# A graph network on one core: the matrix build tile by tile, two (later three) node ranges a tile, and relation weights and gathers moved

## The reference

```python
dst = jnp.minimum((6250 * jax.random.uniform(...) ** 2.0).astype(jnp.int32), 49999)   # then sorted
# layer 0: attention over the edges of a node, weighted by a relation weight
z = h @ W.T
rel_alpha = rel_emb[etype, 0]                       # 40 relations
h_agg = segment_sum((rel_alpha * alpha)[:, None] * z[src], dst)
# layer 1: mean over neighbours
summed = segment_sum(node_feature[src], dst)
# layer 2, three times: weighted sum over neighbours
agg = segment_sum(x[src] * w[:, None], dst);  out = agg @ W_rel.T + b_rel + x @ W_root.T
# layer 3: sum over neighbours of h[col] * mlp(edge_rbf)
```

## Time and profile before

| | us |
|---|---|
| median of 3 runs (lowest to highest) | 11397.75 (11381.71 to 11407.65) |
| the profiled execution | 11385.68 |
| its span, from the first to the last instruction | 11384.1 |

### The profile page before, as it was taken

One profiled execution on the slowest core, in us unless ns is written; L12 is line 12 of the kernel. 1 busy time (PEld: TensorE's weight loads), 2 busy tenths in 40 slices (PEclk: granted clock), 3 DMA queues, 4 the chain that ended last, 5 costly groups with the idle time before them and its releaser, 6 DMA issues. The chain is left out here.

```text
span 11384.1 us, 169604 instructions
## 1 busy us (share of the span) xinstructions
PE 7768.9 (68%) x40442; PEld 4847.1 (43%) x40443; DVE 4764.8 (42%) x10974; ACT 2337.1 (21%) x4276; POOL 4043.9 (36%) x4338
## 2 busy tenths in 40 slices
PE   1466666666666565555557999999977777777575
PEld 1222222222323354444443444444455555555565
DVE  7765554444333466555554357000121122222455
ACT  0001111222222455555541000000011111111000
POOL 2677776777661000000000000000047777777100
PEclk8899999999999756666668999999977777777899
DMA  1233444555554433222225777777733333333343
GB/s 48 70 105 125 137 147 161 170 183 183 192 193 154 136 113 104 96 92 89 84 81 199 282 279 289 282 289 287 294 111 116 117 119 117 118 116 113 122 139 123
DMA packets 537811, 1758.10 MB, mean 154 GB/s; under 512 B 96112, under 2 KB 286555, under 8 KB 494020
## 3 DMA queue, kind: packets, MB, share of 16 engines
q1 hardware_dynamic: 374136, 1331.26, 33.8%
q0 software_dynamic: 160032, 421.72, 12.0%
q10 hardware_dynamic: 3312, 1.94, 0.1%
HBM read 1223.40 MB, written 531.19 MB: 154 GB/s over the span
## 5 line engine op out<-in xcount | busy, mean ns | idle before, releaser
L849 PE MATMUL wide<-ring 128*128 x9424 | 2039.8, 342 | 1445.8 <-issue 891.0
L748 POOL DMA_INDIRECT z_got<-z_table,z_idx x1568 | 1837.9, 1172 | 698.6 <-issue 384.2
L849 PEld LDWEIGHTS wide<-ring 128*128 x9424 | 917.9, 97 | 2351.1 <-issue 2092.4
L1756 POOL DMA_INDIRECT sorted_rows<-l_rows,l_idx x1568 | 1553.9, 991 | 603.9 <-issue 439.9
L1384 PE MATMUL wide<-stream,X 128*128 128x512 f32 (+1 forms) x2548 | 1042.2, 569 | 60.1 <-DMA stream<-c_dense 57.9
L385 PE MATMUL wide<-rows,onehot 128*128 128x130 f32 x3904 | 877.1, 413 | 226.0 <-DVE A L402 225.7
L793 DVE TENSOR_TENSOR ring<-iota_h,src_r 128x512 bf16<-128x512 f16 (+1 forms) x394 | 272.7, 692 | 1720.0 <-PE wide L849 1702.7
L1003 POOL DMA_DIRECT2D rows<-z_edges x196 | 103.4, 528 | 2399.5 <-PE wide L374 2069.3
L1645 PE MATMUL wide<-H,l_onehot_t 128*128 x3904 | 547.5, 275 | 595.9 <-DVE l_rows L1718 529.1
L385 PEld LDWEIGHTS wide<-rows,onehot 128*128 128x128 f32 x3904 | 808.7, 314 | 289.0 <-DVE A L402 285.9
L1384 PEld LDWEIGHTS wide<-stream,X 128*128 128x128 f32 x2548 | 467.4, 191 | 600.6 <-issue 540.2
(11 more groups left out here) (275 smaller groups left out, 9797.2 us busy)
## 6 DMA issues: line engine op xcount, KB each, us to landing
stream<-w_dense SPq DMA_DIRECT2D x252, 1792.0 KB, 7.5
stream<-c_dense SPq DMA_DIRECT2D x84, 1792.0 KB, 7.5
z_edges<-z_got POOLq DMA_DIRECT2D x392, 264.0 KB, 2.7
rows<-z_edges POOLq DMA_DIRECT2D x196, 528.0 KB, 3.9
l_rows<-sorted_rows SPq DMA_DIRECT2D x196, 516.0 KB, 3.4
dst_bc<-in_dst_row SPq DMA_DIRECT2D x196, 512.0 KB, 3.7
l_dst_bc<-in_dst_row SPq DMA_DIRECT2D x196, 512.0 KB
c_dense<-A SPq DMA_DIRECT2D x49, 1568.0 KB
```

Of the source, the lines that this page charges most:

```text
L748: e.indirect_dma_start(out=z_got[:, s, t, :], out_offset=None, in_=z_table, in_offset=bass.IndirectOffsetOnAxis(ap=z_idx[:, s, t:t + 1], a ...
L849: ins = e.matmul(pairs[k][:, 512 * (m > 0):512 * (m > 0) + WC], lhsT=ring[:, bass.ds(rows_at + m * P, P)], rhs=ring[:, bass.ds(cols_at, WC ...
L1756: e.indirect_dma_start(out=sorted_rows, out_offset=bass.IndirectOffsetOnAxis(ap=idx[:, s, t:t + 1], axis=0), in_=rows[:, s, t, 0:MW], in_o ...
```

## The change

- **Matrix build.** The order is now by tiles. In a turn of eight tiles TensorE goes through the eight slots at fixed places; the window of the tile before (`base_tab`, eight numbers loaded a turn) says into which of the four PSUM windows it multiplies. Each tile is multiplied with two ranges of 392 columns in the first three quarters of the turns (147 of 196), with three in the last quarter, whether or not it has edges there. The PSUM windows start from zeros that ScalarE writes (`clear`) after each copy; the closing matmuls are gone from this loop, and ScalarE waits for the number of tiles done. VectorE writes 784 instead of 1176 columns a tile in the first three quarters.
- **The flag of the mending** gets a new formula: the count, less 1 where the window's first tile is in the last quarter, is compared with SPAN - 3.
- **Relation weights** leave the prelude and `l0z`; VectorE sums one relation in each of the first 40 turns of the build.
- **z gathers** go by groups of eight tiles in two buffers; the first 14 groups move from the build to the ranging block.

```diff
-NO_COLS = 4 * P + SPAN * WC
-SLOT = NO_COLS + WC
+SLOT = 4 * P + SPAN * WC
+TRIPS = NT // RING
+WIDE_TRIPS = TRIPS * 3 // 4
...
-            if b < DVE_RELS - EARLY_RELS:
-                add_relation(e, b + EARLY_RELS, mask, rel, False)
...
-                for r in range(DVE_RELS, N_RELS):
-                    add_relation(e, r, mask_pool, rel_pool, r == DVE_RELS)
...
-                e.tensor_tensor(rel[:, :], rel[:, :], rel_pool[:, :], ALU.add)
...
+            with e.Fori(lo, hi) as i:
+                for s in range(2):
+                    g = i * 2 + s
+                    with e.If(i > 0):
+                        e.wait_ge(s_zput[s], i * 16)
+                        e.sem_inc(note["pool"], 1)
+                    e.tensor_copy(z_idx[:, s, :], src_i[:, bass.ds(g * TILES, TILES)]).then_inc(s_zidx, 1)
+                    e.wait_ge(s_zidx, g + 1)
+                    e.sem_inc(note["pool"], 1)
+                    for t in range(TILES):
+                        e.indirect_dma_start(
+                            out=z_got[:, s, t, :], out_offset=None, in_=z_table,
+                            in_offset=bass.IndirectOffsetOnAxis(ap=z_idx[:, s, t:t + 1], axis=0),
+                        ).then_inc(s_zgot[s], 16)
...
+            @block.gpsimd
+            def _(e):
+                gather_pairs(e, 0, EARLY_PAIRS)
...
-                e.tensor_scalar(step[:, :], same[:, :], float(SPAN - 1), None, ALU.is_gt)
+                e.tensor_scalar(step[:, :], first_tile[:, 0:NW], float(WIDE_TRIPS * RING), None, ALU.is_ge)
+                e.drain()
+                e.tensor_tensor(step[:, :], same[:, :], step[:, :], ALU.subtract)
+                e.drain()
+                e.tensor_scalar(step[:, :], step[:, :], float(SPAN - 3), None, ALU.is_gt)
...
+                with e.Fori(0, N_RELS) as i:
+                    make_tiles(i, SPAN - 1)
+                    e.tensor_scalar(rel_mask[:, :], type_f[:, :], rel_id[:, bass.ds(i, 1)], rel_row[:, bass.ds(i, 1)],
+                                    ALU.is_equal, ALU.mult)
+                    e.drain()
+                    e.tensor_tensor(rel[:, :], rel[:, :], rel_mask[:, :], ALU.add)
+                with e.Fori(N_RELS, WIDE_TRIPS) as i:
+                    make_tiles(i, SPAN - 1)
+                with e.Fori(WIDE_TRIPS, TRIPS) as i:
+                    make_tiles(i, SPAN)
...
+                def add_tile(i, k, spans):
+                    e.wait_ge(s_made, i * RING + (k + 1))
+                    e.sem_inc(note["pe"], 1)
+                    e.reg_add(gone, bases[k], spans)
+                    e.wait_ge(s_gone, gone)
+                    e.sem_inc(note["pe"], 1)
+                    for v in range(spans):
+                        if v:
+                            e.reg_add(into[v], bases[k], v)
+                        e.reg_alu(into[v], into[v] if v else bases[k], 3, op=ALU.bitwise_and)
+                    to = [e.snap(into[v], min_val=0, max_val=3) for v in range(spans)]
                     for m in range(4):
+                        for v in range(spans):
+                            ins = e.matmul(banks[:, bass.ds(to[v], 1), int(m > 0), 0:WC].rearrange("p a x -> p (a x)"),
+                                           lhsT=slots[:, k, m * P:(m + 1) * P],
+                                           rhs=slots[:, k, 4 * P + v * WC:4 * P + (v + 1) * WC],
+                                           start=False, stop=False, skip_group_check=True)
                     ins.then_inc(s_room, 1)
...
                         for n in range(HB // WN):
-                            e.wait_ge(s_win, i * (2 * HB // WN) + (k * (HB // WN) + n + 1))
+                            e.wait_ge(s_room, e.snap(ends[n], min_val=1, max_val=NT + RING))
                             e.sem_inc(note["act"], 1)
-                            e.copy(staging[k][:, :, :, WN * n:WN * (n + 1)], window(n % 4)).then_inc(s_gone, 1)
+                            e.copy(staging[k][:, :, :, WN * n:WN * (n + 1)], window(n % 4))
+                            e.drain()
+                            clear(n % 4)
```

More of the change, by code:

```diff
@@ L191, in build_program @@
         spread_f = sb("spread_f", [PARTS * TILES, GE], of=prelude)
[L192 to L205, removed]
         s_small, s_edge, s_w = sem("s_small"), sem("s_edge"), sem("s_w")
@@ L251, in _ @@
                 e.memset(one_f[:, :], 1.0)
+                e.memset(zero_f[:, :], 0.0)
                 e.wait_ge(s_small, 32)
@@ L580, in _ @@
                 e.drain().then_inc(s_run, 1)
[L581 to L584, removed]
+                e.memset(base_tab[:, 0:1], 0.0)
+                e.tensor_copy(base_tab[:, 1:NT], runs[:, 0, 0:NT - 1])
                 e.drain()
[L586 to L600, removed]
+                e.tensor_scalar(base_tab[:, 1:NT], base_tab[:, 1:NT], 3, None, ALU.arith_shift_right)
                 e.wait_ge(s_wid, 32)
@@ L835, in _ @@
             def _(e):
-                slot, cols, made, skip, wrap, behind, step, more = (e.alloc_register("bd_pe_" + n) for n in (
-                    "slot", "cols", "made", "skip", "wrap", "behind", "step", "more"))
+                slot, made, gone, turned = (e.alloc_register("bd_pe_" + n) for n in ("slot", "made", "gone", "turned"))
+                bases = [e.alloc_register(f"bd_pe_base{k}") for k in range(RING)]
+                into = [e.alloc_register(f"bd_pe_into{v}") for v in range(SPAN)]
@@ L838, in _ @@
                 regs = range_registers(e, "bd_pe")
-                coded = [e.alloc_register(f"bd_pe_coded{k}") for k in range(4)]
-                others = e.alloc_register("bd_pe_others")
-                assert NT < 2048
-                before = e.alloc_register("bd_pe_before")
-                LAST = RING * SLOT
-                def add_tile(k, first):
-                    rows_at = e.snap(slot, min_val=0, max_val=LAST - SLOT)
-                    cols_at = rows_at + e.snap(cols, min_val=4 * P, max_val=NO_COLS)
-                    for m in range(4):
-                        ins = e.matmul(pairs[k][:, 512 * (m > 0):512 * (m > 0) + WC],
-                                       lhsT=ring[:, bass.ds(rows_at + m * P, P)], rhs=ring[:, bass.ds(cols_at, WC)],
-                                       start=(first and m < 2), stop=False)
-                    ins.then_inc(s_room, 1)
@@ L869, in other_tiles @@
-                def other_tiles():
-                    e.reg_alu(more, others, 1, op=ALU.min)
-                    e.reg_mul(step, more, SLOT)
-                    e.reg_mul(cols, more, SPAN * WC)
-                    e.reg_alu(cols, no_cols, cols, op=ALU.subtract)
-                    e.reg_alu(others, others, 1, op=ALU.max)
-                def close_window(k, s):
-                    for h in range(2):
-                        ins = e.matmul(pairs[k][:, 512 * h + 511:512 * h + 512], lhsT=zero_h[0:1, :], rhs=one_col[0:1, :],
-                                       start=False, stop=True)
-                    ins.then_inc(s, 1)
@@ L914, in _ @@
+                for lo, hi, spans in ((0, WIDE_TRIPS, SPAN - 1), (WIDE_TRIPS, TRIPS, SPAN)):
+                    with e.Fori(lo, hi) as i:
+                        e.load(bases, base_tab[0:1, bass.ds(i * RING, RING)])
+                        for k in range(RING):
+                            add_tile(i, k, spans)
                 e.wait_ge(s_gone, NW + 4)
```

179 lines of the change are left out of this document (66 added, 113 removed).

## The result

The changed kernel takes 24,167.46 us (median of 4 runs, 24,161.78 to 24,181.38) against 11,393.51 us before (median of 4, 11,381.71 to 11,407.65): the ratio is 2.121, with a 95% interval of 2.118 to 2.125. The forecast was 24,400 us, slower, in a range of 23,500 to 25,400. The profiled execution has a span of 24,179.8 us. Lines of the changed kernel have other numbers: the tile loop's matmul is L834, a mended tile's L864, the mending's DMAs L718.

What follows compares the result with a forecast made beforehand. It took the build to be bound by TensorE's sequencer, at 2356 tile turns of about 1.4 us. Start 320 + tile loop 2700 + mending 13,800 + last stores about 5 + later layers 7,580 = 24,400 us, range 23,500 to 25,400.

Steps and rivals of the forecast that it cites:

- The flag: Mending: windows with count 1 exceed the new limit 0, so 784 windows are mended instead of one.
- rival (a): Mending: the flag stays clear, for instance because the scan's count starts one lower; 10,620 us, chance 0.04.
- A round: Mending: serial chain, fixed 13.6 us a window plus 1.31 us a tile; 13,800 us in all, bounds 13,050 to 14,700.
- Rival (b): Mending: a steady stream of its DMAs takes longer than the single round of before; chance 0.06.
- Rival (c): Mending: a round is shorter, address work hidden or code warm after the first; 1.5 us less, 23,200 us, chance 0.06.
- The loop's start: Before the tile loop: 355 - 8 - 118 + 90 = 319, so the loop starts at 320 us.
- the block of z: Before the build: without waits for relation sums and mask it takes 35 us for 153.2, so 118 us come back.
- lower bound for this block: Ranging block: early gathers take 182 us, block +90, bounds +60 to +120, the lower by gathers VectorE does not disturb.
- The tile loop: Matrix build: 1.5 us a two-range tile, 2.05 a three-range tile; 2700 us in all, ends 2330 and 3590.
- half of the per-turn cost: Tile loop: load and branch of some 0.8 us per 8 tiles, half of it counted, entered as 130 us.
- ScalarE now clears a window after each copy: Tile loop: copy and clear, 2 x 0.81 us, against at least 2 tiles of TensorE; claimed hidden.
- The rest: Three later layers behind the build: not touched by the change, taken over at 7,580 us.

Runs made afterwards that it cites:

- run 1: Changed kernel with only the flag's limit at SPAN - 2 instead of SPAN - 3: 10,509.02 us, ratio to before 0.924.
- run 3: Changed kernel, mending writes c_dense only, 7 instead of 14 DMAs a round: 20,464.94 us.
- run 4: run 1 with EARLY_PAIRS = 0, so no z gathers in the ranging block: 10,422.89 us, ratio to before 0.916.
- run 12: run 1 with ScalarE's clear of a window after each copy left out, output not the same: 11,087.43 us on the fourth chip.
- runs 9 and 11: Kernel before with 109 or 64 semaphore increments ahead of VectorE's layer-0 edge loop: 11,742.87 and 11,741.97 us, against 11,915.09.
- run 10: run 1 with 19 semaphore increments more on VectorE ahead of layer 0's edge loop: 11,189.25 us, 34 packets.

## Why the prediction was right, step by step

**The flag.** Right, and the whole sign of the result: 10,976 DMAs for 14, and the time of rival (a), a clear flag, shows up in run 1 as 10,509 us where 10,620 was worked out. With the limit at 0 the flag rises and at 1 it does not, so the largest count less correction is 1. By the counts worked out from dst, a scan that started one lower would have given 0 there and a clear flag: the scan does count an unshared first tile as 1.

**A round.** Fixed 13.6 us + 2 x 1.31 = 16.2 us was the sum; 16.21 us is what the timeline has. One round in the trace of before, read link by link, was enough. Total 13,690 us for 13,800 predicted, inside 13,050 to 14,700. Rival (b), with 0.06 in the prediction's chances, was a steady stream of such DMAs that takes longer than the single round of before; it is refuted: seven issues take 4.04 and 4.15 us where all 14 took 8.3, and the DMA share over the stretch is 0.34. In the page 10.09 million of the changed kernel's 10.53 million packets are under 512 bytes, and their rate was not what bound the loop: by the share of 0.34 the DMA engines were idle two thirds of the time, and with half the packets (run 3) only 0.50 us a round went from the wait for landing, against 4.25 from the issue. The loop was bound by issue and by the wait for landing. Rival (c), a shorter steady round, is refuted by the same 16.21 us.

**The loop's start.** 305 us for 320. The parts: the block of z lasted from 34.9 to 66.8 us, 32 us for 35, the ranging block took 175 us (83.5 to 258.5) for 182, and GpSimd ended it. Within a group a gather came every 1.25 us (86.61, 87.88, 89.13) where 1.62 had been read with the wait for indices in it; with index copy and waits a group of eight took 12.5 us for 13.0, so the reading was good. (The prediction's lower bound for this block supposes that VectorE slows a gather; no run tested that. The gathers of the changed kernel took 0.94 to 3.45 us, half of them under 0.98.) Run 4 shows the price of the early gathers: 86 us, and nothing came back for them, since the gathers weren't late later either.

**The tile loop.** 2790 us for 2700, and this is the term with an error in it, two of them with opposite signs. The sum 1764 + 804 + 130 has 130 us for "half of the per-turn cost"; half of 196 turns of 0.8 us is 78, so the sum by its own words was 2,646. Taken as written, 0.66 us a turn, it gives the two-range part 1862 us, and 1792 came (1.52 us a tile): 70 less. The three-range part gets 836, 2.13 us a tile, and took 998, 2.55 a tile: 162 more. The step that failed is "ScalarE now clears a window after each copy: 2 x 0.81 us against at least 2 tiles of TensorE, hidden". That compared rates (ScalarE has time enough) and not the latency: with four windows and three of them in use by a tile, there is a single spare one, and the tile after next needs it copied, cleared and handed over. In the rows above the first tile of the pair from 2702.63 ends at 2704.70; then come the copy (from 2704.91, 0.81), the clear (from 2705.79, 0.81) and 0.91 us from the clear's end to the next matmul at 2707.51. That is 2.81 us, one tile of 2.07 us covers it, and the rest is the gap of 0.73. Run 12 shows it by taking the clear away: 0.26 to 0.31 us a tile of the 0.42 that were missing. The remainder was not traced to a cause.

**The rest.** 7,580 us were taken over as they stood, since no line behind the build was changed; 7,394 came. The layer-0 loop is 200 us shorter, with 240 packets of instructions fewer; moving VectorE's code alone does the same to the kernel before (runs 9 and 11), which makes it the likely cause here (run 10 did not confirm it). The forecast had no term for this, and none of its range came from it.

**How the errors stand.** -15 in the start, +90 in the loop, -109 in the mending, -5 for last stores that cost nothing apart, -186 behind it: -225 us, from 24,405 (the sum before it was rounded) to 24,180. The agreement to 1% is a large term well measured, and not small terms all right; that they partly cancel is luck. In a forecast for run 1's kernel the 186 us would be a fifth of the gain.

## What to carry to other kernels

When a change touches a comparison that guards a rare path, work out its value from the data before anything else, and price that path from the one pass that the trace has, link by link; here 1 in a limit was worth 13,660 us, and an 8% gain lay hidden under it. For buffers in a ring, compare the latency of free-and-refill with the work of the tiles that cover it, not the rates of the engines. When an untouched loop changes its time, look at the packets of instructions before looking for contention, and move the code of each engine in turn to test it. And compare versions on one chip only, or stage by stage.

## What the runs showed of the hardware

- **Instructions ahead of a loop that do nothing saved 172 us.** In the kernel before, 240 packets of 8.2 KB (2.24 MB in 274) are moved on the instruction queue beside a loop of 49 turns, and with 64 or 109 semaphore increments ahead of VectorE's loop they are gone; in the changed kernel they are absent with and without 19 increments. Each turn of before then has a wait of up to 3.9 us with releaser "issue", where the longest is 1.8 without the packets. With 64 increments the kernel was 1.5% faster (11,741.97 for 11,915.09 us, one run of each).
- **Chips differ, and in few stages.** The same kernel before took 11,378, 11,815, 11,915 and 11,915 us on four chips, 4.7% apart, while repeated runs on the first two agree to about 0.2%. The traces put almost all of it in one loop, layer 3's over the edges: from the first to the last of VectorE's writes of l_rows it took 2154 to 2159 us in the traces of the first chip, 2605 to 2622 on the second, 2686 to 2708 on the third and 2704 on the fourth. The edge loop of layer 0, the products with c_dense and w_dense (2204 to 2210 us everywhere) and the build of the kernel before (3431 us from the first to the last of TensorE's tile matmuls on the first chip, 3434 on the second, 3437 and 3452 on the third) differ by some 20 us at most. The denser tile loop of run 1's code does differ: 2786, 2854 and 2950 us on the first three. Its traces from the slower chips have waits that the first chip's has not among its longest (VectorE's L767 with the releaser "remote", 34 to 89 us in all between 2150 and 2950 us). The cause stays open.
- **Idle time "issue" can be a wait.** Most of the 0.7 us gaps in TensorE's rows, which run 12 showed to be for the most part a wait for ScalarE's clear, are put down to "issue": the clear had ended 0.9 us before the matmul started. That the sequencer's register work behind the wait fills this time fits, but is not shown.
